# Second context attention's output projection: rows 6 and 7 of both halves in the last two units, token tile by token tile

## What is computed

```python
x = x + _L0_xattn_ref(_layernorm(x), ctx_4096, ...)            # 16 heads of 96
x = x + _L0_attn_ref(_layernorm(x), ...)                       # causal, 16 heads of 64
x = x + _L0_ffn_ref(_layernorm(x), route_w, A, Bw)             # low-rank, one of 8
x = x + _L1_xattn_ref(_layernorm(x), ctx_4096, ctx_4096, ...)  # 32 heads of 32, 8 key heads
x = x + _L1_attn_ref(_layernorm(x), ...)                       # causal, 32 heads of 32
x = x + _L1_ffn_ref(_layernorm(x), ...)                        # 8-bit integers, width 2752
```

```python
out = jnp.einsum('bhqk,bhkd->bhqd', probs, v)
out = out.transpose(0, 2, 1, 3).reshape(b, sq, DIM)
return out @ Wo            # 256 x 1024 times 1024 x 1024
```

## Time and profile before

| | |
|---|---|
| median of 3 runs | 2008.74 us (2005.05 to 2013.07) |
| the profiled execution, own time | 2009.56 us |
| its span, first to last instruction | 2008.2 us |
| TensorE busy | 1860.0 us, 93% of the span |
| VectorE, ScalarE, GpSimd busy | 64%, 48%, 26% |
| mean granted TensorE clock | 0.964 |
| mean DMA rate | 150 GB/s |

### The profile page before, as it was taken

The page is one execution under the profiler, slowest core; times in us unless marked ns, Lnnn a source line. Parts: engine busy times, 40 slices in busy tenths (PEclk is TensorE's granted clock), DMA queues, the critical chain, the costliest instruction groups (busy, mean ns, idle before and its releaser), DMA issues.

```text
span 2008.2 us, 28607 instructions
## 1 busy us (share of the span) xinstructions
PE 1860.0 (93%) x11468; PEld 1349.1 (67%) x11468; DVE 1282.0 (64%) x1504; ACT 959.9 (48%) x1431; POOL 520.6 (26%) x243
## 2 busy tenths in 40 slices
PE   6899999999998999999998987989999999979888
PEld 6899999999997877777787865523333333367543
DVE  4566666665453567887656775757777776156765
ACT  4311133333321777767774351046777667734421
POOL 4100022323200003313100000046777777600000
PEclk9999999999999999999999999979999999988989
DMA  6555688877545568978424526623432321037033
GB/s 239 190 158 169 187 275 230 301 195 247 181 130 145 184 152 225 254 176 212 131 75 146 169 73 153 170 59 83 90 90 67 85 69 33 17 104 276 2 153 124
DMA packets 183939, 302.19 MB, mean 150 GB/s; under 512 B 44077, under 2 KB 117857, under 8 KB 175841
## 3 DMA queue, kind: packets, MB, share of 16 engines
q1 hardware_dynamic: 183809, 300.38, 51.7%
HBM read 232.56 MB, written 64.54 MB: 148 GB/s over the span
## 4 chain that ended last, share of the span: by engine, by line
PE 76%; DVE 14%; ACT 4%; issue 3%; DMA 2%; SPq 1%; POOL 0%; ACTq 0%; DVEq 0%
PE psum L703 11%; PE psum L1915 8%; PE psum L1932 6%; PE psum L684 4%; PE psum L686 4%; PE psum L685 4%; PE psum L671 4%; PE psum L1948 3%; PE psum L302 3%; DVE top L2106 3%; PE psum L304 3%; PE psum L303 3%; PE psum L1896 3%; PE psum L1129 3%; PE psum L1114 2%
## 5 line engine op out<-in xcount | busy, mean ns | idle before, releaser
L2106 DVE TENSOR_REDUCE top<-psum 128x4 f32<-128x2048 f32 (+1 forms) x146 | 294.1, 2026 | 102.4 <-PE psum L1896 102.2
L2031 ACT ACTIVATE probs_f<-psum 128x512 f32<-128x512 f32 x512 | 278.5, 594 | 141.3 <-PE psum L1915 129.1
L2176 POOL TENSOR_TENSOR added<-probs_f 128x1024 f32<-128x1024 f32 x126 | 299.1, 2375 | 171.4 <-ACT probs_f L2031 123.7
L878 DVE TENSOR_REDUCE top<-psum 128x2 f32<-128x512 f32 x272 | 184.8, 690 | 160.3 <-PE psum L671 160.1
L1187 DVE TENSOR_TENSOR probs_low<-probs,probs_high 128x1024 fp32r<-128x1024 f32 x136 | 198.0, 1458 | 127.7 <-ACT probs L1149 127.4
L1915 PE MATMUL psum<-q_rows,k_rows 97*128 97x512 f32 x512 | 197.8, 462 | 2.4 <-DMA q_rows<-t_high 1.7
L1915 PEld LDWEIGHTS psum<-q_rows,k_rows 97*128 97x128 f32 x512 | 80.9, 191 | 173.4 <-ACT probs_f L2031 159.1
L684 PE MATMUL psum<-c_high,w_high 128*128 128x256 f32 (+1 forms) x672 | 190.7, 284 | 2.7 <-DVE c_low L841 2.7
L685 PE MATMUL psum<-c_low,w_high 128*128 128x256 f32 (+1 forms) x672 | 190.4, 283 | 0.0
L686 PE MATMUL psum<-c_high,w_low 128*128 128x256 f32 (+1 forms) x672 | 190.4, 283 | 0.0
L1148 ACT ACTIVATE probs_high<-psum 128x1024 fp32r<-128x1024 f32 x136 | 139.5, 1026 | 84.6 <-PE psum L1116 79.5
(11 more groups left out here) (406 smaller groups left out, 3699.9 us busy)
## 6 DMA issues: line engine op xcount, KB each, us to landing
staged<-in_ctxT_dram SPq DMA_DIRECT2D x32, 512.0 KB, 5.5
wf_rows<-in_ffn_w_dram SPq DMA_DIRECT2D x32, 512.0 KB, 6.3
k_four<-k_high SPq DMA_DIRECT2D x128, 128.0 KB, 3.3
wf_rows_c<-in_ffn_w_dram SPq DMA_DIRECT2D x26, 512.0 KB, 4.3
wf_turned_c<-in_ffn_t_dram SPq DMA_DIRECT2D x24, 512.0 KB, 8.1
panel<-in_wo_dram SPq DMA_DIRECT2D x10, 1024.0 KB, 5.9
gate_up<-q_dram SPq DMA_DIRECT2D x10, 1024.0 KB, 7.7
xnT_ab<-in_ffn_t_dram SPq DMA_DIRECT2D x18, 512.0 KB, 6.3
```

The costliest lines, as they stand in the source:

```text
L878: dve.tensor_reduce(top0[:, r0:r0 + 2, n], psum[:, bank, :].rearrange("p (i n) -> p i n", i=2), AX_X, ALU.max).then_inc(*b.bank_read.up())
L2031: act.activation(probs[:, n % 6, half * BANK:(half + 1) * BANK], psum[:, half, :], ACT.Exp, scale=scale).then_inc(*f.exped.up())
L2106: dve.tensor_reduce(top1[:, first:end, t, chunk], psum[:, MAXIMA + first:MAXIMA + end, :], AX_X, ALU.max).then_inc(*f.max_read.up())
L2176: pool.tensor_tensor(added[pair % 4][:], probs[:, n % 6, :], probs[:, (n + 1) % 6, :], ALU.add).then_inc(*f.added.up())
```

## The change

The order of the eight units becomes `WO1_ORDER`: (half, k) = (0,0), (0,2), (0,4), (1,0), (1,2), (1,4), (0,6), (1,6). The weights are laid out for it, each panel in one piece. TensorE runs the first six units whole and then, for each of the two token tiles, that tile's six matmuls of unit 6 and that tile's six of unit 7 (`pe_unit_tile`). ScalarE's splits of units 2 and 3 stand ahead of the four moves of the last head, that of unit 4 ahead of `oT_high`, that of unit 5 behind it, and then the dummy Sqrt and the rest. VectorE splits units 2 to 7 without additions between, then adds both halves of the first tile and both of the second. WQ_B + 0's low part goes behind the layernorm in front of WQ_B + 1's. The number of matmuls, splits, additions and bytes is the same.

```diff
+WO1_ORDER = ((0, 0), (0, 2), (0, 4), (1, 0), (1, 2), (1, 4), (0, 6), (1, 6))
...
+        def pe_unit_tile(u, k, stationary, banks, t, last):
+            high_w, low_w = unit_pair(u)
+            pe.wait_ge(*s.unit_split.at(u + 1))
+            o, ts = psum[:, banks[t], :], slice(t * P, (t + 1) * P)
+            for r in range(2):
+                at = slice(r * BANK, (r + 1) * BANK)
+                high, low, ready = stationary[k + r]
+                if ready and t == 0:
+                    pe.wait_ge(*ready)
+                pe.matmul(o, high[:, ts], high_w[:, at], start=k + r == 0, stop=False)
+                pe.matmul(o, high[:, ts], low_w[:, at], start=False, stop=False)
+                done = pe.matmul(o, low[:, ts], high_w[:, at], start=False, stop=last and r == 1)
+            if t == TT - 1:
+                done.then_inc(*s.unit_read.up())
+            elif last:
+                done.then_inc(*s.row_made.up())
...
-                dve_split(u_q + (3 if ahead == 4 else 1))
+                for u in (3,) if ahead == 4 else (0, 1):
+                    dve_split(u_q + u)
...
-                pe_linear(oT, WO1, 2, (0, 1, 4, 5), True)
+                for u, (half, k) in enumerate(WO1_ORDER[:6]):
+                    pe_unit(WO1 + u, k, oT, (4 * half, 4 * half + 1), False)
+                for t in range(TT):
+                    for u, (half, k) in enumerate(WO1_ORDER[6:], 6):
+                        pe_unit_tile(WO1 + u, k, oT, (4 * half, 4 * half + 1), t, True)
...
                 upper(KV1 - 1, SUMS)
+                act_split(WO1 + 2)
+                act_split(WO1 + 3)
                 for g in range(G1):
                     move_output(KV1 - 1, g)
+                act_split(WO1 + 4)
                 outputs_high(KV1 - 1)
-                act_output(WO1, KT // 2, 2, WQ_B + 2)
+                act_split(WO1 + 5)
+                act.activation(tiny[:, 7, 0:1], ident[:, 0:1], ACT.Sqrt)
+                for u in range(WO1 + 6, WQ_B + 2):
+                    act_split(u)
...
-                dve_output(3, WO1, KT // 2, 2, WQ_B + 2, (0, 1, 4, 5))
+                for u in range(WO1 + 2, WO1 + 8):
+                    dve_split(u)
+                for half in range(2):
+                    dve.wait_ge(*s.row_made.at(3 + half))
+                    dve_add_to_x(half, 0, 4 * half)
+                for half in range(2):
+                    dve.wait_ge(*s.unit_read.at(WO1 + 7 + half))
+                    dve_add_to_x(half, 1, 4 * half + 1)
```

More of the change, by code:

```diff
@@ L102, in panel_plan @@
     halved("wq1", KT, P, False)
-    halved("wo1", KT, P, True)
+    for p in range(4):
+        plan.append((a["wo1"][p], 4 * BANK, P, True))
     halved("wq_b", KT, P, True)
@@ L1664, in vector_program @@
                     low_set(n)
-                dve_output(2 if name == "d" else 4, u_o, KT // 2, ahead, upto, (0, 1, 2, 3))
+                dve_output(2 if name == "d" else 5, u_o, KT // 2, ahead, upto, (0, 1, 2, 3))
             def gpsimd_program():
@@ L2546, in layouts @@
         a[name] = tiled(w, 512)
+    halves = a["wo1"].reshape(2, P_, KT, 512)
+    units = [halves[half, :, k:k + 2, :].reshape(P_, 1024) for half, k in WO1_ORDER]
+    a["wo1"] = c(np.stack([np.concatenate(units[p:p + 2], axis=1) for p in range(0, 8, 2)]))
     a["wkv_b"] = np.concatenate([tiled(i["L1_attn_Wk"], 256)[0], tiled(i["L1_attn_Wv"], 256)[0]], axis=1)
```

## The result

The changed kernel took 1996.9 us in the median of 14 runs, the kernel before, run beside it, 2006.3 (14 runs). The ratio is 0.9950, with a 95% interval of 0.9933 to 0.9967: between 6.6 and 13.4 us less, 9.4 by the medians. The forecast gain, 8.15 us, lies between these. The forecast time, 2000.6, was 3.7 us too high, and the range, 1997.0 to 2004.0, missed the median by 0.1 us.

What follows compares the result with a forecast made beforehand. TensorE, busy 93%, bounds the kernel through idle and slow stretches in the second output projection. By parts 4.6 + 2.5 + 1.4 - 1.2 = 7.3; to the aggregate 8.15 us, from 2008.74 to 2000.6 us, range 1997.0 to 2004.0.

Steps and rivals of the forecast that it cites:

- All three losses: Projection: 4.93 us idle ahead of unit 2, unit 2 2.50 us longer at lower clock, 1.19 us idle at unit 5.
- The term of 2.50 us: Unit 2 of the projection: at full clock it takes 2.78 instead of 5.28 us, once the idle ahead shrinks.
- the new idle ahead of unit 7: Projection's end: unit 7's first tile waits 1.23 us for its low half, with no slower matmuls after it.
- Unit 4 did not wait: Projection's middle: unit 4's split, behind the copies on ScalarE, ends just in time, with 0.1 us of cover.
- Two splits behind the layernorm: VectorE after the layernorm: two splits fit before the first xnT_low with 0.06 us cover; excess costs up to 1.22 us.
- the later tables: SyncE queue: cosine, sine and mask tables come 1.15 us later; cover falls from 1.9 to 0.7 us, costing nothing.
- The last head's delay: Last head's copies and low part, behind moved splits, end near 1769.7 us; 5.7 us of cover hides the delay.
- A: Unit 2's split: GpSimd's product starts before VectorE, costing 1.3 us; gain 6.85 us, 2001.9 us; chance 0.14.
- B: ScalarE's round with the copies does not fit, unit 4 waits up to 2.15 us; gain 6.0, 2002.7 us; chance 0.06.
- D: Next stage: tables land late and the fourth query unit waits; a 12 us delay gives 2011.9 us; chance 0.02.
- E: Unit 2 waits as before for VectorE's inversions; without the clock's 2.5 us, gain 5.6, 2003.1 us; chance 0.04.
- C: Behind the stage, 1826 to 1850 us at clock 0.76: half the lost time goes; gain 11, 1997.7 us; chance 0.14.

Runs made afterwards that it cites:

- filled_gap: Kernel before plus twenty 512-column matmuls nobody reads between units 1 and 2; 31.48 us from first projection matmul to aggregate, one run of 1993.0 us.
- whole_last: Changed kernel with units 6 and 7 run whole, one after the other, additions in unit order; median 1994.9 us, ratio 0.9944 to the kernel before.
- splits_only: Kernel before with only ScalarE's high halves of units 2 and 3 moved ahead of the last head's four moves; median 1996.7 us, ratio 0.9957.
- warm_tuned: Changed kernel, units 6 and 7 whole, unread matmuls at the second context attention's start, fewer ahead of the maxima, another bank; 1995.6 us, ratio 0.9944.
- warm_start: Changed kernel plus some twenty unread matmuls in TensorE's waits at the second context attention's start, low-parts wait moved earlier; 1997.6 us, ratio 0.9967.
- warm_whole: Changed kernel with units 6 and 7 whole and the first placement of unread matmuls at the second context attention's start; 1997.4 us, ratio 0.997.
- product_first: Changed kernel with VectorE waiting for GpSimd's last normalising product before splitting unit 2; 28.94 us from first projection matmul to aggregate, one run of 2008.5 us.

## Why the prediction was right in the stretch and missed the time

**Bound and mechanism: right.** All three losses were where the prediction saw them, and went as it said. Idle ahead of unit 2 was forecast as 0.3 and is 0.42 us; unit 2 at 6.17 us after the first matmul, measured 6.25; unit 6 at 17.29, measured 17.47; the idle ahead of unit 7 1.23, measured 1.08; the last matmul's end at 24.24, measured 24.54; the aggregate at 25.75, measured 26.03. The 0.3 us missing are unit 2's start, 0.08 late, and the first matmul behind each of the two idle stretches: unit 2 takes 2.88 us instead of 2.78, unit 7's first tile 1.49 instead of 1.39.

**The clock: right in kind, too large in size.** The term of 2.50 us was unit 2's excess over 2.78 us in the one trace at hand. In filled_gap against that trace it is 2.4, against the mean of four traces of before 1.8. That the new idle ahead of unit 7 would leave the clock alone rested on the single stretch of 1.19 us in before. It did so in all seven traces that have it (1.08 or 1.09 us), but the last section shows one of 1.17 us elsewhere that was followed by a fall.

**Covers: right.** Unit 4 did not wait. Two splits behind the layernorm cost 0.05 us, the later tables nothing. The last head's delay was hidden. With VectorE first, GpSimd's product took 2.33 us, as said. What the prediction did not ask is whether the ending tile by tile pays at all: it counted the new idle as the price, and whole_last is 0.66 us faster without it.

**Rivals.** A, GpSimd first, did not occur in any trace of the unaltered changed kernel; its mechanism was right, but it was priced at 1.3 us, and forced by a wait it cost 2.9, because the clock fell behind the longer idle. B, D and E fell. C, more than the stage gives, put the time at 1997.7, closer than the forecast did. The place it named does not bear it out: in the 24 us from 34.7 us behind the aggregate the granted clock is 0.74 to 0.88 in the four traces of before and 0.75 to 0.77 in the four of the changed kernel.

**The time: missed, mostly by the base.** The step that failed is the base in "for the median I say **2000.6 us**", which is 2008.74, the median of three runs, less 8.15. These three are the first of the fourteen, whose median is 2006.3: 2.4 of the 3.7 us missed. The fourteen have a standard deviation of 4.2 us, so a median of three carries some 2.9 us by estimate, not the "some 2 us" of the prediction. Before measured 2006.3, 2005.2, 2002.9, 2007.0 and 2005.2 us in its five sets of 14 to 26 runs, and the profiled execution, at 2009.6, was high too, with a projection that started 3 to 6 us later than in the other traces of before. With 2006.3 the forecast would have been 1998.2, inside the range. The other 1.3 us are gain beyond 8.15, and no stretch explains them: four traces of before, with 33.0 twice, 33.3 and 33.9, put the stretch's mean gain at 7.3, under the forecast. That the gain of 8.15 lies so near the 9.4 measured is therefore in part luck.

**What stays open.** The three comparisons of the unaltered changed kernel give ratios of 0.9950, 0.9945 and 0.9946 and 9.4, 9.4 and 8.0 us by the medians, where the stretch shows 7.0 to 7.9, in the mean 7.3. Each interval alone reaches down to some 7 us. Taken together they do not: the 27 runs of the changed kernel are faster than the 57 of before beside them by 9.8 us in the mean, and an estimate of the 95% interval from their scatter is 1.7 us to either side. So some 2 us more than the stretch are likely, and where they arise is not shown. The spans in the table differ by 9.7 us in the mean of four traces each: 7.3 are the stretch, 1.65 an earlier start of the projection and 0.7 the rest, but the starts of one kernel alone lie up to 5.7 us apart. The altered kernels don't settle it, since splits_only, whole_last and warm_tuned gain more than their stretches give, warm_start and warm_whole less.

## What to carry to other kernels

Look at what stands ahead of a stalled engine's supplier in its own in-order queue: here two splits that needed nothing from the last head stood behind its five copies, and moving them alone gave 6.3 of the 7.3 us. Price an idle stretch of TensorE as the wait plus the slower matmuls that may follow it, from more than one trace, and check the order of starts where VectorE and GpSimd both read SBUF. Build a forecast on a stretch measured from its own first instruction, and take the base time with the spread that the runs show, on both sides.

## What the runs showed of the hardware that was not expected

The length of one idle stretch did not decide whether TensorE's clock fell behind it. In the projection, 1.77 us was followed by 0.50 in product_first, and 1.1 to 1.2 us by 1.00 in all thirteen traces that have it. Elsewhere in the first trace of before, 1.17 us was followed by a fall and 2.55 us was not (for each, the row of the matmul behind the idle stretch, then a stretch with length, TensorE busy, clock, DMA share, GB/s):

```profile
1332.84 0.54 PE L1896 MATMUL psum<-k_four,q_nat_high 32*128 32x512 f32 x4 [1.17 <-DVE top L2106]
...
1334.00:1336.00 2.00, 2.00 (x10) 0.50 0.00 0
```

```profile
1242.02 0.44 PE L1762 MATMUL psum<-ident,hidden_e 128*128 128x128 f32 x2 [2.55 <-DVE hidden_e L1804]
...
1242.02:1246.00 3.98, 3.50 (x9) 1.00 0.88 179
```

And TensorE can stay at 0.50 while it is busy without a gap: 4.00 of 4.00 us in the rows of before at 1318 to 1326 us, where most matmuls use 32 rows or 32 columns of the array. The changed kernel's trace has the same matmuls at 1.00 there, so their shape alone does not hold the clock down.
